# Writing out TensorE's four looped rounds in a two-layer transformer kernel

## The reference

```python
x = x + ln(attn0(ln(x)))   # 16 heads of 16, rope, causal softmax, Wo and bias
x = x + ln(ffn0(ln(x)))    # silu(x Wg^T) * (x Wu^T), then Wd^T; hidden width 768, integer weights / 127
x = x + ln(attn1(ln(x)))   # 16 heads of 64, 50*tanh(s/50), causal softmax, Wo
x = x + ln(ffn1(ln(x)))    # mixes each token with the one before; sigmoid(xr Wr^T) * (relu(xk Wk^T)^2 Wv^T)
```

## Time and profile before

| | |
|---|---|
| three timed runs | 1541.90, 1548.32, 1549.69 us |
| profiled execution, its own time | 1542.39 us |
| its span, first to last instruction | 1540.7 us |
| mean granted TensorE clock in the span | 0.975 of full speed |
| TensorE (PE) busy | 1430.6 us, 93% |
| VectorE, GpSimd, ScalarE busy | 70%, 53%, 52% |
| layer 0's four looped rounds on TensorE | about 240 to 565 us of the span |
| layer 1's four looped rounds on TensorE | 970.7 to 1379.9 us of the span |

### The profile page before, as it was taken

The page is one execution under the profiler, slowest core; times in us unless marked ns, Lnnn a source line. Parts: engine busy times, 40 slices in busy tenths (PEclk is TensorE's granted clock), DMA queues, the critical chain, the costliest instruction groups (busy, mean ns, idle before and its releaser), DMA issues. The chain is left out here.

```text
span 1540.7 us, 32997 instructions
## 1 busy us (share of the span) xinstructions
PE 1430.6 (93%) x12438; PEld 1052.8 (68%) x12438; DVE 1077.7 (70%) x2036; ACT 800.7 (52%) x1132; POOL 814.1 (53%) x1003
## 2 busy tenths in 40 slices
PE   5788989899999999999999999999999999999996
PEld 3555757676676767677776777776767776777765
DVE  6779686877787877775648557666486586675765
ACT  2444444443435344645666666655665565666651
POOL 4233534353544445425757576575585575756652
PEclk8889999999999999999999999999999999999999
DMA  5111120212121113020100010100100001000000
GB/s 188 59 60 57 56 70 22 84 42 82 41 82 41 69 42 114 26 69 29 35 29 2 1 43 1 42 2 2 42 1 20 24 1 43 1 1 29 1 29 14
DMA packets 45768, 61.42 MB, mean 40 GB/s; under 512 B 3760, under 2 KB 31312, under 8 KB 45648
## 3 DMA queue, kind: packets, MB, share of 16 engines
q1 hardware_dynamic: 44784, 59.03, 11.3%
q10 hardware_dynamic: 864, 0.66, 0.2%
HBM read 25.83 MB, written 8.39 MB: 22 GB/s over the span
## 5 line engine op out<-in xcount | busy, mean ns | idle before, releaser
L1689 ACT ACTIVATE l_probs<-psum 128x1024 f32<-128x1024 f32 (+1 forms) x192 | 164.6, 879 | 144.7 <-PE psum L1957 120.7
L905 ACT ACTIVATE l_probs<-psum 128x512 f32<-128x512 f32 x256 | 138.1, 594 | 174.8 <-PE psum L1172 172.3
L987 DVE TENSOR_REDUCE l_rowmax<-psum 128x2 f32<-128x1024 f32 (+2 forms) x192 | 159.0, 863 | 38.9 <-PE psum L1133 38.4
L298 POOL TENSOR_TENSOR l_pool_holder<-expo 128x1 f32<-128x1 f32 x128 | 31.9, 249 | 291.8 <-ACT l_probs L1695 199.8
L303 POOL TENSOR_SCALAR_AFFINE_SELECT l_probs<-l_probs 128x256 f32<-128x256 f32 (+1 forms) x384 | 181.4, 503 | 0.0
L1764 DVE TENSOR_TENSOR l_qk_lo<-psum,l_qk_hi 128x1024 fp32r<-128x1024 f32 x64 | 77.9, 1217 | 134.0 <-ACT l_qk_hi L1679 133.7
L1695 ACT ACTIVATE l_probs<-l_probs 128x2048 f32<-128x2048 f32 (+1 forms) x128 | 161.5, 1268 | 0.5
L1773 DVE RECIPROCAL l_keysum<-psum 128x256 f32<-128x256 f32 x64 | 112.2, 1753 | 65.0 <-PE psum L1986 64.5
L2000 PE MATMUL psum<-l_probs,l_v 128*32 128x512 f32 (+3 forms) x2048 | 152.4, 437 | 0.8 <-DVE l_att L1786 0.7
L1786 DVE TENSOR_TENSOR l_att<-psum,l_keysum 64x256 f32<-64x256 f32 x256 | 107.9, 422 | 20.0 <-PE psum L2000 12.8
L2000 PEld LDWEIGHTS psum<-l_probs,l_v 128*32 128x32 f32 x2048 | 63.8, 110 | 84.9 <-issue 73.1
(11 more groups left out here) (212 smaller groups left out, 4172.2 us busy)
## 6 DMA issues: line engine op xcount, KB each, us to landing
l_kT<-l_roped_hi SPq DMA_DIRECT2D x32, 256.0 KB, 2.5
l_qT<-l_roped_hi SPq DMA_DIRECT2D x32, 256.0 KB, 2.6
l_xin<-in_x SPq DMA_DIRECT2D x8, 512.0 KB, 4.4
l_kT<-l_roped_lo SPq DMA_DIRECT2D x16, 256.0 KB, 2.8
l_qT<-l_roped_lo SPq DMA_DIRECT2D x16, 256.0 KB, 2.5
l_x<-in_x SPq DMA_DIRECT2D x8, 512.0 KB, 3.6
x_mid<-l_x SPq DMA_DIRECT2D x8, 512.0 KB, 3.1
l_xin<-x_mid SPq DMA_DIRECT2D x8, 512.0 KB, 4.4
```

The source lines that it names most:

```text
L905: space.free(nc.scalar.activation(probs[:, SLOT[p], e, c0:c1], space.unit(*use), ACT.Exp, scale=HD0 ** -0.5), *use)
L987: reduced = nc.vector.tensor_reduce(rowmax[:, a // 2, :, a % 2, t], space.unit("max", a, k)[:, :, c0:c0 + (t + 1) * P], mybir.AxisListType ...
L1689: space.free(nc.scalar.activation(probs[:, p % 2, :, c0:c1], space.unit("score", p, u)[:, :, 0:c1 - c0], ACT.Tanh, scale=HD1 ** -0.5 / CLA ...
```

## The change

TensorE's program alone no longer has a loop: its rounds 3 to 6 are written out in both layers, with an integer `j`, in the order that the loop had. The other four engines keep their loops. Every matmul, its operands and its order stay as they were. The counts of TensorE's waits become constants, and the part of its program that stood once for four rounds stands four times.

```diff
-    def loop(self, eng, pieces):
-
-        with eng.Fori(self.lo, self.hi + 1) as j:
-            for piece in self.order:
-                if piece[0] in pieces:
-                    pieces[piece[0]](j - self.shift[piece], *piece[1:])
+    def round(self, j, pieces):
+        for piece in self.order:
+            if piece[0] in pieces:
+                pieces[piece[0]](j - self.shift[piece], *piece[1:])
+
+    def loop(self, eng, pieces, unrolled=False):
+
+        if unrolled:
+            for j in range(self.lo, self.hi + 1):
+                self.round(j, pieces)
+        else:
+            with eng.Fori(self.lo, self.hi + 1) as j:
+                self.round(j, pieces)
...
-        schedule.loop(eng, pieces)
+        schedule.loop(eng, pieces, unrolled=eng.engine == nc.tensor.engine)
```

## The result

| | kernel before | changed kernel |
|---|---|---|
| median of the timed runs | 1549.01 us (4 runs, 1541.90 to 1549.72) | 1537.16 us (4 runs, 1534.10 to 1539.02) |
| ratio of after to before, 95% interval | | 0.9932 (0.9904 to 0.9961) |
| profiled execution: own time, span | 1542.39, 1540.7 us | 1534.10, 1532.4 us |
| mean granted TensorE clock in the span | 0.975 | 0.974 |

The changed kernel is 0.7% faster: 11.9 us in the medians, 8.3 us between the two profiled executions. Lines of the kernel stand 7 further down now: the `score` of L1957 is L1964, L1986 is L1993, L2028 is L2035, L424 is L431, L202 is L209. The loop's L108 is L117.

What follows compares the result with a forecast made beforehand. PE, busy 93% of the span, was taken as the bound, with stops at layer 1's loop edges. 9.5 + 4.3 + 0.4 + 1.1 = 15.3 us off 1548.3 gives 1533.0, said as 1532 for possible third-edge low clock; range 1522 to 1541.

Steps and rivals of the forecast that it cites:

- Three taken branches in layer 1: TensorE's loop edges in layer 1: their idle time goes, worth 9.5 us, bounds 0 and 9.6.
- A: Rival: the edges' idle time comes back as PE's waits for ACT, DVE and POOL; 1542.5 us, chance 0.11.
- E: Rival: something other than the branch holds the first `score` of layer 1's rounds and stays; 1547 us, chance 0.02.
- The low clock behind them: TensorE's half clock behind layer 1's edges goes with the idle time; worth 4.3 us, bounds 0 and 4.9.
- The waits themselves: TensorE's waits with an integer `j` ask for the same counts as the loop's form; put at nothing.
- 0.4 for branches: Layer 0's three taken branches go, about 0.15 us each: 0.4 us together, 0.8 at most.
- 1.1 for registers: Register arithmetic on TensorE's sequencer goes: zero in layer 1, 1.1 us in layer 0, bounds 0 and 7.6.
- Rival C: Every register instruction of layer 0's claims' line is on PE's path: 7.6 us go, 1525.5 us, chance 0.08.
- The longer program: Layer 0 must fetch about 17 instruction packets, layer 1 about five fewer; fetched ahead, costed at nothing.
- B: Rival: layer 0's 17 new packets come late, up to 56 us added, 1588 us; chance 0.03.
- D: Rival: the buffer holds only a short stretch, so layer 0's taken branches stop TensorE too; 1522 us, chance 0.01.
- this case: Low-clock stretches move and multiply behind layer 0's waits; each worth 1.6 to 3.4 us, two held in the range.

Runs made afterwards that it cites:

- e3: Kernel before with both TensorE loops kept and a hint on them that announces the branch back; 1531.60 us, 0.9898 of the kernel before.
- e2: Kernel before with TensorE's rounds written out in layer 0 alone, layer 1 looped as before; 1546.97 us, 0.9996 of the kernel before.
- e9: Changed kernel with the two waits of layer 1's `score` and `x3_T` in the other order; 1533.73 us, 0.9919 of the kernel before.
- e1: Kernel before with TensorE's rounds written out in layer 1 alone, layer 0 looped as before; 1535.20 us, 0.9917 of the kernel before.
- e4: Changed kernel with each written-out TensorE round inside a loop of one pass; 1533.92 us, 0.9905 of the kernel before.

## Why the prediction was right, and where its sizes were off

The time, 1537.16 us, lies in the range of 1522 to 1541 and 5 us above the forecast of 1532. The mechanism, the stop of TensorE at layer 1's branch, was the right one. What was off is the size of two terms: the form of the waits, put at nothing, and layer 0's 1.5 us. By its own steps:

**Three taken branches in layer 1, 9.5 us: right.** The idle stretches are gone and did not come back as waits (A). In the round from 1072 to 1171 us PE's waits for others sum to 0.6 + 0.6 + 0.4 + 0.3 = 1.9 us, where e3, looped, has 1.7. e3 takes the stop away and keeps the loop, which shows that the stop was the branch's (E falls).

**The low clock behind them, 4.3 us: right.** The granted clock is 1.00 over 970:1372 us. That the third edge can have low clock too is borne out: e2's does, 6.8 us from 1280.9 us on. A round without either costs 98.85 us (e3), as the one round of before that I took for it did, 98.84.

**Layer 1 in all: 13.8 forecast, 12.1 measured.** The step that failed is "The waits themselves ask for the same counts ... Nothing". The counts are the same, but the form isn't: of two waits for one load, the written-out program puts the one that is last in the code in front of the load, and here that is the late one. It costs 1.7 us in four rounds by the difference to e3, and e9 takes most of it back.

**Layer 0: a gain of 1.5 us forecast (0.4 for branches, 1.1 for registers), none measured.** The branches cost what I said (e1: 210 ns taken, 76 at the end). The term that failed is the 1.1 us for registers: the 0.3 us in 75 that no other engine accounted for did not go with them. Round 4 has 6.8 us at clock 0.50 in both profiles of the pair and takes 81.45 us before, 81.73 us after: 0.3 us more, with the cheaper branch already in it. Three places in it, where such a pair of waits costs 0.08 to 0.09 us more when written out, account for most of that. This is read from traces, not tested by itself. The 1.1 us that the profiled pair loses in layer 0 also has 3.4 us more of low clock in it, so it is no measure of the form. Rival C has no support: its 7.6 us lie outside e2's interval. But since e4 didn't separate the registers, they are shown to be free only in layer 1, where e3 keeps them all at 98.85 us.

**The longer program, nothing: right.** 16 packets came in layer 0 where I said some 17, and none was late. B is refuted by e2, which has the straight code of layer 0 and no "issue" wait of PE in its rounds.

**D, every taken branch of a long body stops TensorE: refuted.** Bodies of 1,462 and 1,478 instructions are never brought in again; the stop begins between there and 1,734.

**The profiled time, 1527.1 forecast, 1534.1 measured.** Of the 7.0 us, 1.6 are layer 1 (a gain of 13.8 forecast, 12.2 by the cut above), 2.7 are layer 0 and what follows it (-1.5 forecast, +1.2 measured), and 2.7 stood ahead of the first looped round, where the code is unchanged. That last part is luck of the two executions: in the profiles of the experiments that start with the same code, the low clock ahead of that loop sums to between 37.5 and 54.6 us, and the profile of the kernel before has the lowest of these sums.

**Signs that did not come.** PE's busy time was to fall by 4 us and rose by 1.8; layer 0 was to be 0 to 4 us shorter and was 1.1 longer; the first round of layer 1 took 99.5 us where 98.8 to 99.3 stood. The first two go with the low clock, of which the other parts of this execution had more. The prediction named this case last and held two such stretches to be inside its range.

## What to carry to other kernels

Before writing out a loop for its branch, look at the duration of the taken branch and at the instruction packets of a pass: 0.2 us and no packets mean there is nothing to win (layer 0), some 3.6 us and packets in every pass mean there is. Then try the hint on the branch back first, and only on the loop that stops; here it gave all of the gain from one line. Where a load waits for two semaphores and the counts are constants, compare both orders of the waits at the place where one of them is late.

## What the runs showed of the hardware that was not expected

A body whose top is lost without the hint is held whole with it: layer 1's 1,862 instructions, 64 q8 packets in the kernel in place of 91.

In the looped rounds behind the first, layer 0's clock falls at one place of a round, or not at all. Windows of the changed kernel, then of the kernel before:

```profile
372.90:379.70 6.80, 5.59 (x23) 3.08 (x27) 6.56 (x18) 1.08 (x2) 2.83 (x6) 0.50 0.44 149
454.80:461.60 6.80, 5.59 (x23) 3.07 (x25) 6.56 (x18) 1.09 (x2) 2.78 (x6) 0.50 0.46 151
536.70:543.50 6.80, 5.59 (x23) 2.80 (x22) 6.39 (x18) 1.08 (x2) 2.60 (x5) 0.50 0.20 68
```

```profile
454.00:461.00 7.00, 5.83 (x69) 3.43 (x67) 6.76 (x20) 1.58 (x3) 2.35 (x4) 1.00 0.36 121
```

A round with such a stretch takes 81.4 us looped, one without 79.6. That is 1.8 us each. All seven profiles with a looped layer 0 and no padding in it have one round of the four without any; the five with layer 0 written out on TensorE alone have none, but less low clock in the first round, so that the sums are 20.5 to 23.9 us looped and 23.9 to 27.3 written out. What decides whether a place falls was not tested.

Low clock makes most of the scatter between runs of one kernel. The 17 runs of the kernel before beside e1 to e4 go from 1554.45 us at a mean granted clock of 0.965 to 1539.79 us at 0.976, and the time follows the clock through all of them (correlation -0.97). So with times a few us apart, compare the granted clocks first.
